# Routed experts of the first layer: two tables of token sums instead of one

## The chip, the core and the metric

The kernel runs on one core of a Trainium2 chip. The metric is device time of one execution in microseconds (us), the median of the runs shown. Engines are named as in the profile: PE is TensorE's matmul and PEld its weight load, DVE is VectorE, ACT is ScalarE, POOL is GpSimd, SP is SyncE, which only issues DMAs and waits here.

## The reference, cut to what matters

The whole program is a two layer model over 1250 tokens (nodes) of 512 float32 values: in each layer a graph network and a linear attention, then a mixture of experts. The change touches the mixture of experts of layer 0:

```python
gate_probs = softmax(x @ gate_w.T)                 # 1250 x 16 experts
top_v, top_i = top_k(gate_probs, 4); top_v = softmax(top_v)
routed = sum over e of combine[:, e] * (gelu(x @ re_w1[e] + re_b1[e]) @ re_w2[e] + re_b2[e])
shared = mean over 2 shared experts of the same form
x = x + routed + shared
```

Each token goes to 4 of 16 experts, so a token's row of the result is a sum of 4 routed terms, the shared term and the residual.

## The kernel before, in words

`build` runs the stages one after the other. Every stage is a block in which each engine has its own instruction stream, and the next stage begins when all engines have left the block. `stage_experts` is called once per layer; it runs `stage_front` (gate, routing tables, shared experts) and then `stage_routed`, which the change edits.

**Tiles.** The front sorts the token and expert pairs by expert and cuts them into tiles of at most 128 pairs of one expert. In layer 0 there are 48 tiles, numbered g = 0 to 47, in layer 1 there are 28. Buffers of a tile exist twice, by its parity b. Tiles 0, 1 and 2 and the last one are written out; the others run in a hardware loop of two tiles per turn on every engine.

**One tile on PE** (in program order of a turn): `raise_up(g)` (L1930, eight matmul records, first product), `turn_hidden(g-1)` (L1939), `turn(g+1)` (L1920, transposes the gathered rows), `bring_down(g-1)` (L1948, second product). On DVE `bias` (L2022) and `place` (L2015, L2016), on ACT `place_hidden` (L1976), `squash` (L1984) and `weigh` (L1990, writes the weighted result `y[b]`).

**One tile on POOL** is the function `tile(i, g, b)`: it reads two numbers of `landed_by` into registers, waits until the gather into `rows[b]` and the add of tile g-2 (same parity) have landed (`landed[b]`), copies the row numbers of tile g (`know_row`, L1854), issues the gather of the token rows of tile g+4 from the DRAM table `token_rows` (`gather`, L1861, which first waits for `place(g+2)`), then waits on both `landed` semaphores for the adds of all tiles of earlier experts, and issues the add of tile g: an indirect DMA that adds the 128 rows of `y[b]` to rows of the DRAM table `token_sums` (`add_rows`, L1869). Within one expert a token occurs once, so adds of one expert touch different rows; adds of different experts can touch the same row, and two such adds in flight together would lose one. `weigh(g)` on ACT waits for `know_row(g)`, which stands behind `landed[b]`, since both overwrite what the add of tile g-2 reads.

**Weights.** SP keeps a ring of 3 experts. `load_expert` (L878, L879, L882; 512 KB, 128 KB and 512 KB) brings expert e when expert e-3 is done.

**Around the loop.** In `stage_adjacency` the DRAM tables are filled with zeros (L594), SP waits for them (L597). At the end of `stage_front` SP writes residual plus shared experts into `token_sums` (L1040). When POOL has seen the last adds land (`all_added`, L1912), SP reads the table back: in layer 0 into `st.res3` (L1845, 125 partitions by 10 rows of 2 KB), in layer 1 into the output (L1847), and waits for it. In layer 0 the next stage is a layer norm (L276 on DVE, L307 on ACT, L300 on PE).

Of the kernel before, what the change touches and what calls it, by code (L numbers as in the profile page):

```python
# [19 lines left out]
F32 = mybir.dt.float32  # L20
# [6 lines left out]
NODES = 1250  # L27
TS = 125
NT = NODES // TS
D = 512  # L30
# [14 lines left out]
ROW = D + NE  # L45
# [35 lines left out]
def stage_semaphores(nc, ctx, cleared=[]):  # L81


    taken = []
    stage = nc.next_id()

    def sem(name):
        taken.append(nc.alloc_semaphore(name=f"{name}_{stage}"))
        return taken[-1]

    def leave():
        while cleared:
            nc.release_semaphore(cleared.pop())
        for s in taken:
            nc.gpsimd.sem_clear(s)
        cleared.extend(taken)

    ctx.callback(leave)
    return sem
# [751 lines left out]
class L0_EXPERTS:  # L851

    top, shared, shared_weight, swiglu = 4, 2, 0.5, False
    slots, early = P, 3
    ff, blocks, w1_cols = 256, 2, 256
    gate_w, gate_b = "L0_ffn_gate_w", None
# [4 lines left out]
class L1_EXPERTS:  # L861

    top, shared, shared_weight, swiglu = 2, 1, 1.0, True
    slots, early = P, 1
    ff, blocks, w1_cols = 384, 3, 768
    gate_w, gate_b = "L1_ffn_gate_w", "L1_ffn_gate_b"
# [917 lines left out]
def stage_routed(nc, st, ar, kind, ins, rt, out):  # L1784
# [5 lines left out]
    TILES = 2 * rt.most_pairs  # L1790
# [7 lines left out]
    hid = [ar.take(F * P) for _ in range(2)]  # L1798
    ht = [ar.take(F * P).rearrange("p (f n) -> p f n", f=F) for _ in range(2)]
    y = [ar.take(D) for _ in range(2)]  # L1800
    weight = ar.take(TILES)
    own_row = [ar.take(2).bitcast(I32) for _ in range(2)]
    if SW:
# [7 lines left out]
    with ExitStack() as ctx:  # L1811
        sem = stage_semaphores(nc, ctx)
        w1_loaded, w2_loaded, sums_read = rt.w1_loaded, rt.w2_loaded, sem("sums_read")
        rows_turned, xt_placed, rows_used = sem("rows_turned"), sem("xt_placed"), sem("rows_used")
        up_ready, up_biased, hid_ready = sem("up_ready"), sem("up_biased"), sem("hid_ready")
        hid_turned, ht_placed, down_ready, y_made = (
# [4 lines left out]
        landed = [nc.alloc_semaphore(name=f"landed{b}_{kind.top}") for b in range(2)]  # L1821
        block = ctx.enter_context(nc.Block())

        def more_pairs(eng):
            return eng.value_load(rt.pairs[0:1, 0:1], min_val=1, max_val=rt.most_pairs - 1)

        def expert_of(eng, g):
            return eng.value_load(rt.expert_of[0:1, bass.ds(g, 1)], min_val=0, max_val=NE - 1)  # L1828
# [1 line left out]
        def ring_of(eng, g):  # L1830
            return eng.value_load(rt.ring_of[0:1, bass.ds(g, 1)], min_val=0, max_val=R - 1)

        sums = rt.sums

        @block.sync
        def _(sp):
            for e in range(kind.early, NE):
                if e >= R:
                    sp.wait_ge(down_ready, sp.value_load(rt.done_by[0:1, e - R:e - R + 1], min_val=1, max_val=TILES + 1))
                load_expert(sp, rt, kind, ins, e)  # L1840
            sp.wait_ge(w1_loaded, 32 * NE)
            sp.wait_ge(w2_loaded, 16 * NE)
            sp.wait_ge(all_added, 1)
            if out is None:
                sp.dma_start(st.res3, sums[1:NODES + 1, :].rearrange("(t p) d -> p t d", p=TS)).then_inc(sums_read, 16)  # L1845
            else:
                sp.dma_start(out, sums[1:NODES + 1, :]).then_inc(sums_read, 16)  # L1847
            sp.wait_ge(sums_read, 16)

        @block.gpsimd  # L1850
        def _(pool):

            def know_row(b, pair):
                pool.tensor_copy(own_row[b], pair).then_inc(row_copied, 1)  # L1854

            def gather(g, b):

                pool.wait_ge(rows_used, g + 3)
                pool.wait_ge(row_copied, g + 2)
                pool.nop().then_inc(gather_begun, 1)  # L1860
                pool.indirect_dma_start(  # L1861
                    out=rows[b], out_offset=None, in_=rt.table,
                    in_offset=bass.IndirectOffsetOnAxis(ap=own_row[b][:, 1:2].bitcast(mybir.dt.uint32), axis=0)
                    ).then_inc(rows_loaded[b], 16)

            def add_rows(g, b):
                pool.wait_ge(y_made, g + 3)
                pool.nop().then_inc(add_begun, 1)  # L1868
                pool.indirect_dma_start(  # L1869
                    out=sums, out_offset=bass.IndirectOffsetOnAxis(ap=own_row[b][:, 0:1].bitcast(mybir.dt.uint32), axis=0),  # L1870
                    in_=y[b], in_offset=None, compute_op=ALU.add).then_inc(landed[b], 16)

            def tile(i, g, b):
                earlier = [pool.value_load(rt.landed_by[odd][0:1, bass.ds(g, 1)], min_val=16, max_val=16 * TILES)  # L1874
                           for odd in range(2)]

                pool.wait_ge(rows_loaded[b], i * 16 + (48 - 16 * b))
                pool.wait_ge(landed[b], i * 16 + (16 - 16 * b))
                know_row(b, rt.row_of[:, bass.ds(g + AHEAD, 1), :].rearrange("p a w -> p (a w)"))
                gather(g, b)  # L1880
                for odd in range(2):
                    pool.wait_ge(landed[odd], earlier[odd])
                add_rows(g, b)

            pool.nop().then_inc(row_copied, 1)
            for b in range(2):

                pool.wait_ge(rows_loaded[b], 16)
                pool.tensor_copy(first_rows[:, b:b + 1], rt.row_of[:, 2 + b, 1:2]).then_inc(first_copied, 1)
                pool.wait_ge(first_copied, b + 1)  # L1890
                pool.wait_ge(rows_used, b + 1)
                pool.indirect_dma_start(
                    out=rows[b], out_offset=None, in_=rt.table,
                    in_offset=bass.IndirectOffsetOnAxis(ap=first_rows[:, b:b + 1].bitcast(mybir.dt.uint32), axis=0)
                    ).then_inc(rows_loaded[b], 16)
            pool.wait_ge(rt.sums_set, 16 * NT)
            for g in range(2):
                know_row(g, rt.row_of[:, g + AHEAD, :])
                gather(g, g)
                if g:  # L1900
                    pool.wait_ge(landed[0], 16)
                add_rows(g, g)
            tile(0, 2, 0)
            more = more_pairs(pool)
            with pool.Fori(1, more) as i:  # L1905
                for b in (1, 0):
                    tile(i, i * 2 + (2 - b), b)
            tile(more, more * 2 + 1, 1)
            for b in range(2):
                pool.wait_ge(landed[b], more * 16 + 16)  # L1910
                pool.wait_ge(rows_loaded[b], more * 16 + 48)
            pool.nop().then_inc(all_added, 1)  # L1912
# [97 lines left out]
        def _(dve):  # L2010
# [16 lines left out]
            def swiglu(g, b):  # L2027
                e = expert_of(dve, g)
                pairs = biased[b].rearrange("p (n m) -> p m n", m=2)
                lo, hi = own_clamp[b][:, 0], own_clamp[b][:, 1]  # L2030
                dve.tensor_copy(own_act[b], rt.act5[:, bass.ds(e * 5, 5)]).then_inc(mixed, 1)
                dve.tensor_copy(own_clamp[b], clamps[:, :, bass.ds(e * 2, 2)]).then_inc(mixed, 1)
                dve.wait_ge(up_biased, g + 3)
                dve.wait_ge(mixed, g * 4 + 2)
                dve.tensor_scalar(gate[b], pairs[:, 0, :], hi[:, 0:1], lo[:, 0:1], ALU.min, ALU.max).then_inc(clipped, 1)
                dve.tensor_scalar(up[b], pairs[:, 1, :], hi[:, 1:2], lo[:, 1:2], ALU.min, ALU.max).then_inc(mixed, 1)
                dve.wait_ge(sig_ready, g + 1)
                dve.scalar_tensor_tensor(out=sig[b], in0=gate[b], scalar=own_act[b][:, 1:2], in1=sig[b],
                                         op0=ALU.mult, op1=ALU.mult).then_inc(mixed, 1)
                dve.wait_ge(mixed, g * 4 + 4)  # L2040
                dve.scalar_tensor_tensor(out=hid[b], in0=up[b], scalar=own_act[b][:, 2:3], in1=sig[b],
                                         op0=ALU.add, op1=ALU.mult).then_inc(hid_ready, 1)
# [9 lines left out]
            with dve.Fori(0, more) as i:  # L2052
                for b in (1, 0):
                    g = i * 2 + (2 - b)
# [6 lines left out]
            g = more * 2 + 1  # L2061
            bias(g, 1)
            if SW:
                swiglu(g, 1)


DYN = 12534
# [2 lines left out]
def build(nc, ins, out):  # L2070
    with ExitStack() as ctx:
        words = 53200
        whole = ctx.enter_context(nc.sbuf_tensor("arena", [P, words], F32))
        st = State()
# [17 lines left out]
        TABLE = P * (-(-(NODES + 1 + P) // P))  # L2092
        st.table = nc.dram_tensor("token_rows", (TABLE, ROW), F32, kind="Internal").ap()
        st.sums = nc.dram_tensor("token_sums", (TABLE, D), F32, kind="Internal").ap()
        st.made_rows = [(st.table, ROW), (st.sums, D)]
        st.routed_zeroed = nc.alloc_semaphore(name="routed_zeroed")


# [1 line left out]
        ar = Arena(whole, st.counts16_at[0], words)  # L2100
# [19 lines left out]
        ar = Arena(whole, DYN, words)  # L2120
# [14 lines left out]
        ar = Arena(whole, DYN, words)  # L2135
# [34 lines left out]
```

## Time and profile before

| | |
|---|---|
| median of 3 runs | 2692.89 us (2692.82 to 2703.66) |
| profiled execution, its own time | 2696.6 us |
| its span, first to last instruction | 2694.8 us |
| mean granted TensorE clock | 0.935 |
| busy: PE, PEld, DVE, ACT, POOL | 84%, 48%, 36%, 19%, 16% |

The profile shows one execution. Its stretches are read by windows in us from the span's start. The routed experts of layer 0 lie at about 990 to 1303, those of layer 1 at about 2400 to 2695. "Issue" as a releaser means that the engine waited for nothing that the profile shows. A releaser is inferred: a wait for several semaphores is put down to the one that came last. Spans on POOL are rough, and some records of matmuls and of DMA landings are missing.

### The profile page before, as it was taken

Reading aid. Unit: us, or ns where it says so; the run is one execution under the profiler, and the core shown is the slowest. Engines: PE = TensorE matmul, PEld = TensorE weight load, DVE = VectorE, ACT = ScalarE, POOL = GpSimd, SP = SyncE. Lnnn points to the kernel's source line nnn. Section 1 sums busy time; section 2 is a strip of 40 time slices with the busy share of each in tenths; the row PEclk is TensorE's granted clock in tenths of the full one; section 3 lists DMA queues with packets and bytes.
Section 4 is the critical chain, followed back from the end, with each engine's and each line's share of the span. In section 5 each row is a group of like instructions: output and inputs, shape, how many; then the busy total and the mean of one; then the engine's idle time right before and its main releaser. Section 6 shows DMA issues by size and latency. Waiting matters only on the chain. (4 is left out here: it accounts for less than half of the span.)

```text
span 2694.8 us, 27626 instructions
## 1 busy us (share of the span) xinstructions
PE 2270.1 (84%) x7356; PEld 1284.5 (48%) x7357; DVE 971.8 (36%) x2322; ACT 501.8 (19%) x885; POOL 442.6 (16%) x599
## 2 busy tenths in 40 slices
PE   4976775989897898877498698998989988889996
PEld 2532332444444445444244246883458854435553
DVE  4162665420203632211105435531245402624443
ACT  1110122101010302222200014421134302201111
POOL 3995000000000014444100000000000010002332
PEclk9987998999999999999698898998999999989998
DMA  3000200000000326666300000002000010237774
GB/s 109 0 0 0 87 0 16 16 1 16 0 0 0 125 64 161 149 154 134 105 0 0 30 25 1 1 1 85 1 0 1 0 35 22 96 129 207 233 233 126
DMA packets 77350, 159.33 MB, mean 59 GB/s; under 512 B 9219, under 2 KB 20526, under 8 KB 77202
## 3 DMA queue, kind: packets, MB, share of 16 engines
q1 hardware_dynamic: 59602, 115.62, 12.8%
q0 software_dynamic: 17664, 42.64, 7.9%
q8 instruction: 47, 0.77, 0.1%
q14 instruction: 37, 0.30, 0.0%
HBM read 122.06 MB, written 38.74 MB: 60 GB/s over the span
## 5 line engine op out<-in xcount | busy, mean ns | idle before, releaser
L1692 PE MATMUL bank<-arena 125*125 125x257 f32 x1600 | 355.8, 383 | 4.8 <-DVE arena L1611 4.8
L1692 PEld LDWEIGHTS bank<-arena 125*125 125x125 f32 x1600 | 302.2, 189 | 60.5 <-DVE arena L1611 6.3
L1930 PE MATMUL bank<-arena 128*128 x832 | 250.9, 452 | 25.4 <-issue 12.6
L795 PE MATMUL bank<-arena 125*128 125x500 f32 (+1 forms) x720 | 252.6, 512 | 2.3 <-ACT arena L825 2.3
L1930 PEld LDWEIGHTS bank<-arena 128*128 128x128 f32 x832 | 157.0, 194 | 141.3 <-issue 81.8
L1507 PE MATMUL bank<-arena 128*125 128x512 f32 x480 | 211.3, 600 | 9.1 <-DMA arena<-in_L_gnn_W 9.1
L1948 PE MATMUL bank<-arena 128*128 x360 | 177.3, 622 | 36.3 <-ACT arena L1976 27.9
L795 PEld LDWEIGHTS bank<-arena 125*128 125x128 f32 x720 | 135.8, 189 | 120.5 <-issue 110.6
L382 POOL TENSOR_SCALAR arena<-arena 125x125 bf16<-125x125 f16 x320 | 184.4, 760 | 40.7 <-POOLq L266 40.7
L2022 DVE TENSOR_TENSOR arena<-bank,arena 128x384 f32<-128x384 f32 (+1 forms) x104 | 51.5, 496 | 307.8 <-PE bank L1930 296.2
L637 PE MATMUL bank<-arena 125*125 125x500 bf16 x416 | 122.8, 418 | 45.7 <-DVE arena L613 45.7
L1670 ACT ACTIVATE arena<-arena 125x625 f32<-125x625 f32 x160 | 134.5, 900 | 102.5 <-DVE arena L1611 102.3
L429 PE MATMUL bank<-arena 128*125 128x512 f32 x320 | 143.6, 603 | 10.0 <-DMA arena<-in_L_mix_Wqkv 9.3
L1507 PEld LDWEIGHTS bank<-arena 128*125 128x125 f32 x480 | 90.7, 191 | 123.3 <-issue 113.3
L1869 POOL DMA_INDIRECT token_sums<-arena x76 | 121.2, 1595 | 156.8 <-DMA token_sums<-arena 111.9
L613 DVE TENSOR_SCALAR arena<-arena 125x500 bf16<-125x500 f16 x416 | 119.0, 346 | 59.9 <-PE bank L637 53.7
L1611 DVE SCALAR_TENSOR_TENSOR arena<-arena 125x625 f32<-125x625 f32 x160 | 132.4, 864 | 15.8 <-ACT arena L1670 15.8
L777 PE MATMUL bank<-arena 128*125 128x512 f32 x240 | 111.6, 627 | 21.6 <-DVE arena L733 21.6
L752 DVE TENSOR_TENSOR arena<-bank,arena 128x500 f32<-128x500 f32 (+1 forms) x36 | 21.3, 592 | 291.7 <-PE bank L795 291.7
L1543 DVE CUSTOM_DVE_ANT_0 arena<-arena 125x256 f32<-125x256 f32 x160 | 58.6, 421 | 185.7 <-ACT arena L1530 169.3
L1044 POOL MEMSET arena<- 125x20 f32 (+1 forms) x2 | 0.2, 117 | 740.0 <-POOLq L266 740.0
L1739 POOL TENSOR_TENSOR arena<-arena 125x5120 f32<-125x5120 f32 x1 | 11.0, 10999 | 636.5 <-DMA arena<-in_L_gnn_bfc 636.5
(313 smaller groups left out, 2462.8 us busy)
## 6 DMA issues: line engine op xcount, KB each, us to landing
arena<-in_L_ffn_expert_w SPq DMA_DIRECT2D x16, 1536.0 KB
arena<-in_L_ffn_re_w SPq DMA_DIRECT2D x32, 512.0 KB
arena<-in_L_ffn_expert_w SPq DMA_DIRECT2D x16, 768.0 KB
arena<-in_L_ffn_expert_b SPq DMA_DIRECT2D x16, 384.0 KB
token_rows<-arena SPq DMA_DIRECT2D x2, 2500.0 KB
token_sums<-arena SPq DMA_DIRECT2D x20, 250.0 KB
arena<-in_L_gnn_W SPq DMA_DIRECT2D x1, 4096.0 KB, 13.1
arena<-in_L_mix_Wqkv SPq DMA_DIRECT2D x3, 1024.0 KB, 5.3
```

What stands on the lines that cost most here:

```text
L382: pool.tensor_scalar(st.low_marks[:, c, :], st.iota16[:, 0:TS], st.low[:, c:c + 1], None, ALU.is_equal)
L429: last = pe.matmul(out[0:TS, :], st.turned[:, k, i * TS:(i + 1) * TS], w3[:, k, j * D:(j + 1) * D], start=(k == 0), stop=(k == KT - 1))
L613: dve.tensor_scalar(marks[:, u, :], st.iota16[:, 0:WIN * NT], float(w * WIN * NT), st.key[:, bass.ds(col, 1)], ALU.add, ALU.is_equal).then ...
L637: pe.matmul(bank, stays, marks[:, u, :], start=False, stop=False, skip_group_check=True).then_inc(marks_free, 1)
L795: last = pe.matmul(st.bank[4 + n % 4][:, 0:cn], h[:, s, f * P:(f + 1) * P], st.counts[:, s, c0:c0 + cn], start=(s == 0), stop=(s == NT - 1))
L1507: last = pe.matmul(st.bank[n % 4][0:TS, :], x, w[:, k, half * 512:(half + 1) * 512], start=(k == 0), stop=(k == K - 1))
L1611: dve.scalar_tensor_tensor(out=prob[:, u % 2, s, :], in0=excess[:, n % EXCESS, :], scalar=by_one[:, s, head:head + 1], in1=st.counts16[:, ...
L1670: act.activation(excess[:, n % EXCESS, :], row[:, head, d0:d0 + HALF], ACT.Relu, scale=by_fifth[:, s, head:head + 1], bias=minus_one[:, s, ...
L1692: return pe.matmul(st.bank[n % OUTS][0:TS, 0:ONCOL], prob[:, u % 2, s, j * TS:(j + 1) * TS], st.slots[:, head + 1, s, :], start=(s == 0), ...
L1869: pool.indirect_dma_start(out=sums, out_offset=bass.IndirectOffsetOnAxis(ap=own_row[b][:, 0:1].bitcast(mybir.dt.uint32), axis=0), in_=y[b] ...
L1930: last = pe.matmul(st.bank[UP[b][h]][:, 0:WP], xt[b][:, k, :], rt.ring[:, bass.ds(r, 1), k * W + h * WP:k * W + (h + 1) * WP].rearrange("p ...
L1948: last = pe.matmul(st.bank[DOWN[b]], ht[b][:, f, :], rt.ring[:, bass.ds(r, 1), W2_AT + f * D:W2_AT + (f + 1) * D].rearrange("p a n -> p (a ...
```

## The change

`stage_routed` of layer 0 adds tiles of even parity to `token_sums` and tiles of odd parity to a second DRAM table, `more_sums`. Tiles no longer wait for the adds of earlier experts; the wait on `landed[b]` for tile g-2, of the same parity and so of the same table, stays. At the end SP reads both tables in two halves each, and at the end of DVE's stream ten additions put the second table's rows to those of the first. `more_sums` is made and zeroed with the other tables. Layer 1 keeps one table, its waits and its read.

```diff
 class L0_EXPERTS:
...
+    sum_tables = 2
...
 class L1_EXPERTS:
...
+    sum_tables = 1
...
+    more_sums = ar.take(NT * D, TS).rearrange("p (t d) -> p t d", t=NT) if kind.sum_tables == 2 else None
+        half_read = [sem(f"half_read{h}") for h in range(2)]
-        sums = rt.sums
+        TWO = kind.sum_tables == 2
+        sums = [rt.sums, st.more_sums if TWO else rt.sums]
+        HALF = NT // 2
             if out is None:
-                sp.dma_start(st.res3, sums[1:NODES + 1, :].rearrange("(t p) d -> p t d", p=TS)).then_inc(sums_read, 16)
+                for h in range(2):
+                    for b, to in enumerate((st.res3, more_sums)):
+                        sp.dma_start(to[:, h * HALF:(h + 1) * HALF, :],
+                                     sums[b][1 + h * HALF * TS:1 + (h + 1) * HALF * TS, :].rearrange(
+                                         "(t p) d -> p t d", p=TS)).then_inc(half_read[h], 16)
             else:
-                sp.dma_start(out, sums[1:NODES + 1, :]).then_inc(sums_read, 16)
-            sp.wait_ge(sums_read, 16)
+                sp.dma_start(out, sums[0][1:NODES + 1, :]).then_inc(sums_read, 16)
+                sp.wait_ge(sums_read, 16)
...
-                    out=sums, out_offset=bass.IndirectOffsetOnAxis(ap=own_row[b][:, 0:1].bitcast(mybir.dt.uint32), axis=0),
+                    out=sums[b], out_offset=bass.IndirectOffsetOnAxis(ap=own_row[b][:, 0:1].bitcast(mybir.dt.uint32), axis=0),
...
-                earlier = [pool.value_load(rt.landed_by[odd][0:1, bass.ds(g, 1)], min_val=16, max_val=16 * TILES)
+                earlier = [] if TWO else [pool.value_load(rt.landed_by[odd][0:1, bass.ds(g, 1)], min_val=16, max_val=16 * TILES)
                            for odd in range(2)]
...
-                for odd in range(2):
-                    pool.wait_ge(landed[odd], earlier[odd])
+                for odd, tiles in enumerate(earlier):
+                    pool.wait_ge(landed[odd], tiles)
                 add_rows(g, b)
...
-                if g:
+                if g and not TWO:
                     pool.wait_ge(landed[0], 16)
...
+            if out is None:
+                for t in range(NT):
+                    dve.wait_ge(half_read[t // HALF], 32)
+                    dve.tensor_tensor(st.res3[:, t, :], st.res3[:, t, :], more_sums[:, t, :], ALU.add)
...
+        st.more_sums = nc.dram_tensor("more_sums", (TABLE, D), F32, kind="Internal").ap()
-        st.made_rows = [(st.table, ROW), (st.sums, D)]
+        st.made_rows = [(st.table, ROW), (st.sums, D), (st.more_sums, D)]
```

## Rows read from the trace of the kernel before

**Rows 1.** Busy by stretch of the loop: engines, granted clock, DMA share, GB/s.

```profile
core 0: us, PE busy (x) PEld busy (x) DVE busy (x) ACT busy (x) POOL busy (x), PEclk, DMA share, GB/s
1003.80:1264.50 260.70, 212.23 (x810) 128.89 (x810) 52.93 (x135) 65.38 (x136) 126.26 (x136) 0.99 0.67 151
```

**Rows 2.** Waits in 1000:1290: who waited for whom, total us, times, longest.

```profile
POOL token_sums L1869 <- DMA token_sums<-arena: 81.4, 31, 6.7
ACT arena L1990 <- POOL arena L1854: 58.2, 16, 5.3
POOL arena L1861 <- DVE arena L2016: 27.3, 17, 7.2
POOL arena L1854 <- DMA token_sums<-arena: 3.5, 5, 1.6
```

**Rows 3.** Timeline of PE, first product of tiles: start, us, idle before.

```profile
1003.77 1.99 PE L1930 MATMUL bank<-arena 128*128 x8
...
1009.49 1.99 PE L1930 MATMUL bank<-arena 128*128 x8 [0.87 <-issue]
...
1031.12 1.99 PE L1930 MATMUL bank<-arena 128*128 x8 [0.50 <-issue]
...
1036.11 1.99 PE L1930 MATMUL bank<-arena 128*128 x8
...
1199.85 1.99 PE L1930 MATMUL bank<-arena 128*128 x8 [0.21 <-DMA arena<-in_L_ffn_re_b]
...
1208.63 1.89 PE L1930 MATMUL bank<-arena 128*128 x8
...
1237.13 1.99 PE L1930 MATMUL bank<-arena 128*128 x8
...
1264.52 1.99 PE L1930 MATMUL bank<-arena 128*128 x8 [0.74 <-issue]
```

**Rows 4.** Timeline of POOL around one load of weights, with SP's issue of it.

```profile
1041.80 1.59 POOL L1869 DMA_INDIRECT token_sums<-arena  x1 [5.11 <-DMA token_sums<-arena]
...
1045.80 1.60 POOL L1869 DMA_INDIRECT token_sums<-arena  x1 [0.30 <-DMA token_sums<-arena]
1046.83 0.76 POOL L1854 COPY arena<-arena 128x2 int32 x1
...
1052.80 0.37 SPq L878 DMA_DIRECT2D arena<-in_L_ffn_re_w  x1
...
1054.56 1.59 POOL L1869 DMA_INDIRECT token_sums<-arena  x1 [1.03 <-DMA token_sums<-arena]
1055.92 0.43 POOL L1854 COPY arena<-arena 128x2 int32 x1
1058.28 1.01 POOL L1861 DMA_INDIRECT arena<-token_rows,arena  x1 [1.93 <-DVE arena L2016]
1064.54 1.59 POOL L1869 DMA_INDIRECT token_sums<-arena  x1 [5.25 <-DMA token_sums<-arena]
1066.25 0.18 POOL L1854 COPY arena<-arena 128x2 int32 x1
1067.24 1.01 POOL L1861 DMA_INDIRECT arena<-token_rows,arena  x1 [0.80 <-POOL arena L1854]
1068.55 1.60 POOL L1869 DMA_INDIRECT token_sums<-arena  x1 [0.30 <-issue]
```

**Rows 5.** Line L1869, the adds: time from issue to landing where recorded.

```profile
DMA to landing us min/median/max: 4.5/8.5/9.3
```

**Rows 6.** Timeline of the end of the stage, all engines.

```profile
1275.15 1.60 POOL L1869 DMA_INDIRECT token_sums<-arena  x1 [0.30 <-issue]
1280.52 0.33 SPq L1845 DMA_DIRECT2D arena<-token_sums  x1
1303.15 1.28 ACT L307 ACT_TABLE_LOAD   x1 [29.27 <-PEq L1811]
1303.19 1.28 DVE L276 BATCH_NORM_STATS2 arena<-arena 125x6 f32<-125x512 f32 x2 [36.10 <-PEq L1811]
```

**Rows 7.** Transfers in 1281:1304: DMA share in tenths and GB/s, 40 slices.

```profile
DMA  0123333333333333333333333333333333333000
GB/s 21 28 71 114 118 125 132 132 128 125 125 128 135 128 125 125 125 132 132 128 125 125 132 132 128 125 125 128 135 128 125 125 125 132 132 128 118 11 0 0
DMA packets 1255, 2.56 MB, mean 111 GB/s; under 512 B 5, under 2 KB 5, under 8 KB 1255
```

**Rows 8.** Three loads of 500 KB to 125 partitions, issued together; transfers in 1545:1565.

```profile
1543.05 0.41 SPq L1473 DMA_DIRECT2D arena<-in_L_gnn_a_src  x1
1543.51 0.34 SPq L1473 DMA_DIRECT2D arena<-in_L_gnn_a_dst  x1
1543.89 1.54 SPq L1475 DMA_DIRECT2D arena<-in_L_gnn_b  x1
...
DMA  8999999996333333333333333333333320000000
GB/s 328 410 410 410 426 434 418 410 401 279 131 131 131 123 131 131 123 131 131 131 123 131 131 131 123 131 131 123 139 131 131 131 107 25 0 0 0 0 0 0
```

**Rows 9.** Groups of DVE by shape: additions in SBUF, busy us, mean ns.

```profile
L1601 DVE TENSOR_TENSOR arena<-arena 125x500 f32<-125x500 f32 x16 | 10.6, 670 | 0.0
L1249 DVE TENSOR_TENSOR arena<-arena 125x576 f32<-125x576 f32 x1 | 0.8, 759 | 0.1
```

**Rows 10.** Zeroing of the tables: issues with KB and us to landing; SP's waits.

```profile
token_rows<-arena SPq DMA_DIRECT2D x1, 2904.0 KB, 9.5
token_sums<-arena SPq DMA_DIRECT2D x1, 2816.0 KB, 16.3
...
SPq L583 <- PEq L583: 168.3, 1, 168.3
SPq L583 <- DMA token_sums<-arena: 15.0, 1, 15.0
```

**Rows 11.** Gap and restart of PE behind the stage: the same columns as rows 1.

```profile
1281.00:1303.00 22.00, 0.00 (x0) 0.00 (x0) 0.00 (x0) 0.00 (x0) 0.00 (x0) 0.50 0.30 116
1311.00:1330.00 19.00, 13.59 (x76) 11.57 (x76) 4.80 (x11) 9.86 (x18) 0.00 (x0) 0.74 0.47 140
```

## Prediction

> **What bounds the kernel now.** The stage is found first by the lines it uses, then read by windows. Over the loop of layer 0 PE is busy 212 of 261 us, with a few records missing, at a granted clock of 0.99, while POOL is busy 126 and the DMA engines 0.67 [rows 1]. So PE is the engine with the most work, but it isn't full. The table of waits says why not: POOL sat 81.4 us in 31 waits before its adds until earlier adds had landed, and behind it ACT's `weigh` waited 58.2 us in 16 cases for POOL's copy of row numbers [rows 2]. That total is tempting, and it is not the gain. The 81.4 us lie on POOL, which has slack; what counts is how much later PE starts its tiles.
>
> The timeline of PE gives that. The first product of tile 2 starts at 1003.77 and that of tile 47 at 1264.52 [rows 3], 45 intervals in 260.75 us, 5.79 us each. I listed all of them. Thirty-three are 4.87 to 5.85 us long, mean 5.39; the other twelve are 6.16 to 8.78 us and sum to 82.8 us. The longest is 1199.85 to 1208.63, and the last stretch, 1237.13 to 1264.52, has five intervals of 5.48 us on average [rows 3]. The twelve long ones come about once per expert, each behind a stall of POOL of 4 to 6.7 us such as the 5.25 us before the add at 1064.54 [rows 4]. The pattern: SP issues the next expert's weights at 1052.80, the add of the last tile of the expert follows at 1054.56, shares the DMA engines with them, and lands just before 1064.54. The longest recorded landing is 9.3 us [rows 5]. An add without a load beside it is quicker: that of 1041.80 had landed when the copy started at 1046.83, within 5.0 us [rows 4].
>
> **The change part by part.**
>
> *Removed: the wait for earlier experts.* If the long intervals become like the others, the loop takes 45 x 5.39 = 242.6 us, 18.1 less. Taking the last stretch, where no weights come in, 45 x 5.48 = 246.6, 14.1 less. I take 16. The ends: the shortest common interval is 1031.12 to 1036.11, 4.99 us [rows 3]; if every tile ran so, the loop would take 224.6 and the gain would be 36. In most intervals, though, PE idles 0.5 to 0.9 us before L1930 for "issue" [rows 3], which names no wait on POOL. At the other end the gain is nothing. What is late next is PE itself, at about 5.4 us a tile. The two register loads per tile of POOL that go are hidden: POOL needs about 4 us per tile, 1041.80 to 1045.80 [rows 4].
>
> *Kept: the wait for tile g-2.* It stands before the copy of tile g, and the gather of tile g+4, the add of tile g and ACT's `weigh(g)` are queued behind it. With an interval of 5.4 us, the add of g-2 is 10.8 us before the add of g. Behind the copy POOL needs 0.2 us, a pause of 0.8, the gather of 1.0 and a pause of 0.3 before it can add (1066.25 to 1068.55, [rows 4]), 2.3 us. So a landing within 8.5 us costs nothing, and one at 9.3 to 10 us makes the add 0.8 to 1.5 us late once per expert. `weigh` would then be about half a us late, and PE asks for that result one tile later, so most of it is covered. For 13 loads I take 1 us in all, between 0 and 13 x 0.8 = 10 us. Gain: 16 - 1 = 15 us.
>
> *Added: the second table to read, on the path.* Nothing else runs between the last add and the next layer norm. The add at 1275.15 is followed by the read at 1280.52, and DVE starts the layer norm at 1303.19 [rows 6]. In between 2.56 MB move at 125 to 132 GB/s with a DMA share of 0.3 [rows 7]: five of sixteen engines' worth, not all. At 128 GB/s a table takes 20.0 us. The question is whether reads of the second table use the same five. Three loads with the same 125 partitions, issued within a us, show it: once the 16 engine transfer ahead of them is through, they go on at 131 GB/s and a share of 0.3 [rows 8]. They share. So two tables take 40.0 us, 20.0 more. Ends: 0 (if the second ran on other engines) and 20.5 (the rate of the slower slices).
>
> The Trainium skill, page "DMA: Bandwidth & Descriptors", section "Why a DMA increments its semaphore by 16 and not by 1", gives the reason: a DMA issued from SP runs on the largest number up to 16 that divides its slowest dimension, 5 for 125 partitions, and always on the lowest-numbered engines. By that rule, too, all four reads go through the same five, and splitting them in halves wins no rate. The trace agrees with its 0.3 of rows 7 and 8; had the engines been free to choose, this term would be near 0 and the sum negative.
>
> *Added: ten additions on DVE.* Shapes of 125x500 take 670 ns and 125x576 take 759 ns in SBUF [rows 9], so 125x512 takes about 0.69 us. The first five run while the second half of the tables is read, 20 us long; if that cover were gone they would cost 3.5. The last five wait for the last byte: 5 x 0.69 = 3.5 us, plus 0.2 to start. Ends by the two shapes 3.4 and 3.8, with the start 3.4 to 4.2. The SP issues of three more DMAs, 0.33 us each [rows 6], lie under the transfer of the first.
>
> *Added: zeroing.* The second zeroed table landed 6.8 us after the first [rows 10], so a third costs SP some 7 us, at a place where SP afterwards waits 168.3 us for PE. Nobody else waits for it. Cost 0, with 168 us of cover.
>
> *The rest.* Two semaphores more to clear per stage, also in layer 1, whose loop is otherwise the same: 0 to 0.3 us. PE's pause grows from 38 to some 60 us. The clock was already at its lower level of 1.2 GHz (0.50) in this pause, and the restart shows 0.74 on average [rows 11]; a longer pause at the same level should restart alike, 0, at most 1.
>
> **Sum.** Read +20.0, DVE +3.7, loop -15, together +8.7 us. On the profiled execution: span 2694.8 to 2703.5, own time 2696.6 to 2705.3. That execution is 3.7 us above the median of the three runs, so the predicted median is 2692.9 + 8.7, about 2701.5.
>
> **The rivals.**
>
> *The wait for tile g-2 takes the place of the removed one* (slower). Price: up to the whole 16 us; the time would be 2692.9 + 23.7 - (0 to 10), 2707 to 2717. It decides once a landing beside a weight load passes about 10.5 us, or gathers, issued behind the same wait, come too late for PE's transposes. For it: landings of 9.3 and almost 10 us [rows 5, 4], with the 8.5 us of slack already used up, and adds that now follow each other closer. Against it: the DMA engines have a third of their time free [rows 1], and `weigh` has one tile of slack. Chance 0.23.
>
> *PE reaches its own floor.* If the 0.5 to 0.9 us of "issue" before L1930 come from POOL's lateness after all, the gain is between 21 and 36 us: 2680 to 2695. For it: the intervals of 4.9 to 5.0 exist. Against it: the last stretch, without weights in flight, has none. Chance 0.17.
>
> *The second read runs on other engines.* The cost shrinks to 3.7: 2692.9 + 3.7 - 15, some 2682. Against it stand the three loads of rows 8; for it, that reads from DRAM rows aren't broadcasts like those. Chance 0.05.
>
> **How the numbers follow.** The forecast, a gain of 10 to 21 and a cost of 23.7, gives 2695.6 to 2706.6 with chance 0.55. 0.5% of the time, about what a measurement of this kernel can tell from no change, is 13.5 us: bounds 2679.4 and 2706.4. Slower is the first rival, 0.23. Faster needs the far end of PE's floor, or the second read elsewhere with a good loop: 0.04. The rest, 0.73, is within. The range of 2688 to 2714 leaves out the top of the first rival (0.05), the lower half of the second (0.08) and the third (0.05).
>
> **What would show it.** In the changed trace: POOL's wait before L1869 for landed adds gone from 81.4 to some 15 us or less; POOL's copy L1854 waiting for landed adds more than the 3.5 us of rows 2; intervals of L1930 at 5.3 to 5.5 us without the twelve long ones, and the first product of tile 47 about 15 us earlier; from the first read's issue to the layer norm 46 us instead of 22.7, at a DMA share of 0.3 all through; five additions of 0.69 us at its end. It is wrong if the share during the reads is 0.6, if long intervals stay with `weigh` waiting for L1854, or if the loop runs at 5.0 us a tile.

## The result, and the profile after

The changed kernel takes 2716.88 us (median of 7 runs, 2713.06 to 2722.63), the kernel before 2693.59 in its 7 runs. The ratio is 1.0078 with an interval of 1.006 to 1.0095: 16 to 26 us slower, outside the range of 2688 to 2714, where the forecast was 8.7 us slower. The profiled execution of after took 2715.25 us, 18.7 more than that of before; the sum below is made between these two.

The end of the stage took as long as was worked out. Timeline of the kernel after, the last stretch, all engines, to set beside [rows 6]:

```profile
1273.88 0.34 SPq L1855 DMA_DIRECT2D arena<-token_sums  x1
...
1287.69 10.31 SPq L1855 DMA_DIRECT2D arena<-more_sums  x1
1296.57 3.10 DVE L2080 TENSOR_TENSOR arena<-arena 125x512 f32<-125x512 f32 x5 [35.50 <-DMA arena<-more_sums]
1316.80 3.10 DVE L2080 TENSOR_TENSOR arena<-arena 125x512 f32<-125x512 f32 x5 [17.14 <-DMA arena<-more_sums]
1320.17 1.28 ACT L307 ACT_TABLE_LOAD   x1 [52.51 <-PEq L1814]
```

Transfers of after in 1274:1320, share in tenths and GB/s, as in [rows 7]:

```profile
DMA  1233333333333333333333333333333333331000
GB/s 14 77 128 128 128 128 128 126 130 126 128 128 126 126 126 123 125 125 125 126 125 126 130 126 125 128 128 126 123 125 123 125 125 125 125 125 69 0 0 0
DMA packets 2520, 5.12 MB, mean 111 GB/s; under 512 B 20, under 2 KB 20, under 8 KB 2520
```

From the first read's issue to ACT's first instruction of the layer norm it is 1273.88 to 1320.17, 46.3 us, against 22.6 in [rows 6]: 23.7 more, at a share of 0.3 all through. The additions take 0.62 us each, five of them hidden. Up to the second five additions it is 42.9 us (1273.88 to 1316.80), 20.3 more than the whole of before; these additions and the step to ACT add 3.4.

The loop didn't come out as forecast. Timeline of PE, kernel after, the first products (L1942 now), with three neighbours in the middle:

```profile
1002.39 1.99 PE L1942 MATMUL bank<-arena 128*128 x8
...
1019.58 1.99 PE L1942 MATMUL bank<-arena 128*128 x8 [0.94 <-DMA arena<-in_L_ffn_re_b]
1025.19 1.99 PE L1942 MATMUL bank<-arena 128*128 x8 [0.76 <-issue]
1030.94 1.99 PE L1942 MATMUL bank<-arena 128*128 x8 [0.89 <-issue]
...
1258.49 1.99 PE L1942 MATMUL bank<-arena 128*128 x8 [0.98 <-issue]
```

Tile 2 to tile 47 take 256.1 us instead of 260.75 [rows 3]: 4.65 us less, where 15 were forecast. The twelve long intervals are gone, the longest is now 6.0 us. But the short ones are gone too: all 45 lie between 5.27 and 5.99, 5.69 on average. Waits of after in 1000:1285 (engine, tile and line, who ended the wait: us in total, times, longest):

```profile
POOL arena L1873 <- DVE arena L2028: 88.5, 44, 7.0
...
PE bank L1942 <- issue: 26.9, 33, 1.1
...
PE bank L1942 <- DMA arena<-in_L_ffn_re_b: 10.4, 12, 1.1
POOL more_sums L1881 <- DMA token_sums<-arena: 2.9, 3, 1.0
```

POOL's 81.4 us of waiting for landed adds [rows 2] are gone. The 2.9 us listed are three pauses of up to 1.0 us before adds of odd tiles, a place where the changed program has no wait for adds, so that releaser is a wrong guess of the profile; the copy of row numbers, which does stand behind the wait for tile g-2 (L1866 now), isn't listed with any wait for an add. POOL now waits for DVE, which waits for PE. And PE pauses before 45 first products, 37 us in all. Sum of the two profiled executions: before tile 2 -1.4 us, loop -4.65, from the last first product to the read -0.6, read and additions +23.7, behind it +1.6: together +18.65. Outside the stage the code is the same but for the second table's zeroing.

**What PE does in the pause.** Its sequencer reads the next tile's expert and ring place from memory into registers before the first product (`expert_of` L1832, `ring_of` L1835 of after). For one tile, first the add issued ahead of them, from POOL's timeline of after:

```profile
1020.34 1.59 POOL L1881 DMA_INDIRECT more_sums<-arena  x1 [0.98 <-issue]
```

Instructions of L1832 of after in 1022:1024.5 (count: ns min/median/max, first and last start):

```profile
L1832 PEldq TENSOR_LOAD <-arena x1: 935/935/935, 1022.7 to 1022.7; - x1
```

Instructions of L1835 of after in the same stretch:

```profile
L1835 DVEq TENSOR_LOAD <-arena x1: 808/808/808, 1022.8 to 1022.8; - x1
```

A register load mostly takes 0.3 us here. The two that were under way at 1023 took 0.94 on PE and 0.81 on DVE and ended together, at 1023.65, 3.3 us after the start of the add's issue at 1020.34. The next took 0.31. Below are all register loads of PE and DVE in 1000:1285 of each trace, sorted by the time since the start of the last add's issue (long means over 450 ns):

| kernel | begun 2.05 to 2.9 us after an add: long of all | median end of the long ones, us after the add | begun outside 2.0 to 3.3 us: long of all |
|---|---|---|---|
| before | 34 of 38 | 3.31 | 2 of 229 |
| after | 88 of 89 | 3.31 | 0 of 188 |

So a register load of another engine that is under way while an add is some 2.3 to 3.3 us old is mostly held until the add is 3.3 us old. Before, GpSimd's add was delayed by waits of changing length, so the loads met the held stretch sometimes: of the loads ahead of first products of tiles 3 to 47, 18 were long. After, nothing but `weigh` sets the add, and `weigh` follows the second product: the add is issued about 2.5 us before PE's next register load in nearly every tile, and 44 are long. The waits' removal locked the two into the worst phase.

**What a tile of PE is made of.** The intervals alternate, 5.61 and 5.75 above, for a second reason. The loop has two tiles per turn, and ahead of the first of them PE's sequencer goes back to the loop's start. Instructions of L1970 of after in 1024.5:1031, the loop's end between two tiles:

```profile
L1970 PEldq COMPARE_BRANCH  x1: 208/208/208, 1028.3 to 1028.3; - x1
```

If from every interval the time is taken off by which its four PE register loads exceed 0.305 us each, the 22 intervals of after without the loop's end come to 4.98 us (spread 0.01) and the 23 with it to 5.37 (spread 0.03). So PE's pace with these loads in place, and none held, is 5.17 us on average or 233 us for the loop, and the held loads make up the other 23 us of the 256.1. Of the 37 us of pause 23 are the hold, some 9 the loop's end.

**The theories for the runs.** A: this hold sets the pace of 5.7 us. B (rival, that of the prediction): the wait for tile g-2 and the landings set it, and long loads are a sign only. C: PE's sequencer has a fixed overhead, whatever POOL does.

### The profile page after: what moved, and what is told of

Same layout as the page of the kernel before. It is cut to its first block and busy times, and to the rows that moved or that the text cites. A ratio compares the mean times of both kernels' runs of the same rounds, so it can differ in the third digit from the quotient of the medians.

```text
span 2713.4 us, 27231 instructions
## 1 busy us (share of the span) xinstructions
PE 2264.7 (83%) x7356; PEld 1282.4 (47%) x7357; DVE 978.6 (36%) x2332; ACT 502.6 (19%) x885; POOL 444.7 (16%) x599
## 5 line engine op out<-in xcount | busy, mean ns | idle before, releaser
L1942 PE MATMUL bank<-arena 128*128 x832 | 250.6, 451 | 42.5 <-issue 26.9
L1942 PEld LDWEIGHTS bank<-arena 128*128 128x128 f32 x832 | 156.1, 194 | 158.1 <-issue 98.6
L300 PE MATMUL bank<-arena 125*128 125x125 f32 x160 | 26.9, 350 | 111.0 <-DVE arena L290 111.0
```

The source lines that it names most:

```text
L1942: last = pe.matmul(st.bank[UP[b][h]][:, 0:WP], xt[b][:, k, :], rt.ring[:, bass.ds(r, 1), k * W + h * WP:k * W + (h + 1) * WP].rearrange("p ...
```

## The experiments

Times are medians; ratios are to the kernel before on the same chip, whose median was 2693.6 to 2697.8 us. "Loop" is from the first product of tile 2 to that of tile 47 in the profiled execution.

| run | what | ratio (interval) | median us | loop us |
|---|---|---|---|---|
| before | | 1 | 2693.59 | 260.8 |
| after | | 1.0078 (1.006 to 1.0095) | 2716.88 | 256.1 |
| e1_tail_alone | only the second table's read | 1.0103 (1.0081 to 1.0125) | 2723.16 | 262.7 |
| e2_loop_alone | only the loop | 0.999 (0.998 to 0.9999) | 2692.89 | 257.3 |
| e3_numbers_early | after, register loads early | 1.0017 (1.0002 to 1.0032) | 2700.43 | 240.1 |
| e4_before_numbers_early | before, register loads early | 0.9963 (0.9947 to 0.998) | 2685.58 | 255.1 |
| e5_add_later | after, adds delayed | one run | 2737.30 | 269.4 |
| e6_split_reads | after, reads split | 1.0011 (1.0 to 1.0022) | 2699.59 | 257.0 |
| e8_both | after, early and split | 0.9945 (0.9926 to 0.9965) | 2680.88 | 236.4 |
| e9_before_both | before, early and split | 0.9925 (0.9901 to 0.995) | 2677.65 | 253.2 |
| e10_gather_first | e8 with gathers ahead of the wait | 0.9972 (0.996 to 0.9984) | 2689.47 | 248.3 |
| e11_plain_odd | after, odd tiles write plainly | one run | 2699.18 | 243.1 |
| e13_before_gather_first | e9 with gathers ahead of the wait | 1.0011 (0.9991 to 1.0031) | 2701.59 | 276.6 |

### The two halves of the change

e1: waits and the single target of before, with the second table's zeroing, read and additions.

```diff
-                earlier = [] if TWO else [pool.value_load(
+                earlier = [pool.value_load(
-                if g and not TWO:
+                if g:
-                    out=sums[b], out_offset=
+                    out=sums[0], out_offset=
```

> The changed kernel with the waits of before put back and every tile added to the first table; the second table is zeroed, read and added as in the change. The tail theory (four reads of 125 partitions share five engines): from the first read's issue to the layer norm about 46 us instead of 22.7, time 23 to 24 us above before, and the loop as before, tile 2 to tile 47 in 261 us. If the loop's change had cost time of its own, or the larger zeroing did, this would be well under 20 us above before or well over 26.

e2: the loop of the change, the old read.

```diff
-                for h in range(2):
-                    for b, to in enumerate((st.res3, more_sums)):
...
+                sp.dma_start(st.res3, sums[0][1:NODES + 1, :].rearrange("(t p) d -> p t d", p=TS)).then_inc(sums_read, 16)
+                sp.wait_ge(sums_read, 16)
...
-                    dve.wait_ge(half_read[t // HALF], 32)
-                    dve.tensor_tensor(st.res3[:, t, :], st.res3[:, t, :], more_sums[:, t, :], ALU.add)
```

> The changed kernel's loop with two tables, but only the first is read back, in one transfer, and nothing is added on VectorE: the terms of the odd tiles are left out of the result. If the loop gained 4.7 us, as the trace of after has it, the time is 3 to 7 us under before; if the loop had gained the 15 us forecast and something else took it, 15 us under.

e1's profile has 46.3 us from read to layer norm once more (1281.19 to 1327.49) and a loop like before's, 2 us longer. Timed, it is 28 us slower, with an interval of 22 to 34 that takes in the 24 expected. e2 is 0.3 to 5.4 us faster: the loop alone is worth 3 us or so, not 15. Its loop of 257.3 us is after's in the trace, too. The costs are where they were thought to be; the gain is missing.

### Register loads moved

e3: two loads per tile instead of four, into registers kept per parity, ahead of the second product, none ahead of the first.

```diff
+            def fetch(g, to):
+                pe.reg_load(to[0], rt.expert_of[0:1, bass.ds(g, 1)])
+                pe.reg_load(to[1], rt.ring_of[0:1, bass.ds(g, 1)])
...
             def raise_up(g, b):
-                e, r = expert_of(pe, g), ring_of(pe, g)
+                e, r = numbers(b)
...
             def bring_down(g, b):
-                e, r = expert_of(pe, g), ring_of(pe, g)
+                e, r = numbers(b)
...
                     turn(g + 1, 1 - b, i * 16 + 32)
+                    fetch(g + 1, spare)
                     bring_down(g - 1, 1 - b)
+                    for to, new in zip(ahead[1 - b], spare):
+                        pe.reg_mov(to, new)
```

> The changed kernel, with TensorE's two register loads for the next tile moved ahead of the second product and kept in registers, so two loads per tile instead of four, none between the products. Theory A (a register load that is under way 2.3 to 3.3 us after the issue of an add is held until 3.3 us, and with the waits gone this falls on the loads ahead of every first product): the pause of 0.85 us before the first product goes, a tile takes 5.0 to 5.1 us, the loop 225 to 232 us instead of 256, time 24 to 31 us under after. Theory B (the wait for tile g-2 and the landing of adds set the pace, and long register loads are a sign of it only): a tile stays at 5.7 us and the time at after's. The same in layer 1 for both, where up to 10 us more can go.

Timeline of PE, e3 (L1951 is the first product, L1932 the transposes):

```profile
1017.95 1.89 PE L1951 MATMUL bank<-arena 128*128 x8
...
1022.54 1.89 PE L1951 MATMUL bank<-arena 128*128 x8
...
1032.33 1.89 PE L1951 MATMUL bank<-arena 128*128 x8
...
1036.65 0.66 PE L1932 MATMUL bank<-arena 128*128 128x128 f32 x4 [2.21 <-DMA arena<-token_rows,arena]
...
1041.88 1.89 PE L1951 MATMUL bank<-arena 128*128 x8
```

The pause is gone: an undisturbed tile takes 4.59 us, less than the 5.0 that theory A gave, since not only the hold but the loads and the loop's end, too, now lie under the second product. The time falls by 0.6%, some 16 us, less than the 24 to 31 expected. Theory B is out as the pace of after. A next limit shows: six intervals are 7.8 to 9.6 us long, such as 1032.33 to 1041.88. That is why the loop is 240 and not the 225 to 232 expected. Timeline of POOL and SP, e3, at that place:

```profile
1027.93 0.38 SPq L880 DMA_DIRECT2D arena<-in_L_ffn_re_w  x1
1028.89 1.01 POOL L1873 DMA_INDIRECT arena<-token_rows,arena  x1 [0.80 <-POOL arena L1866]
...
1038.80 0.18 POOL L1866 COPY arena<-arena 128x2 int32 x1 [3.01 <-DMA more_sums<-arena]
```

Landing of the gather of 1028.89 (L1873 in 1028.5:1029.5), and all engines in 1038.3:1041.7 (columns as in [rows 1]):

```profile
DMA to landing us min/median/max: 7.7/7.7/7.7
1038.30:1041.70 3.40, 3.23 (x4) 1.51 (x5) 0.00 (x0) 0.00 (x0) 1.19 (x2) 0.50 0.31 51
```

In all six PE waits 1.7 to 2.2 us for gathered rows, as at 1036.65. The gather in question was issued 1.0 to 1.1 us after the next expert's weights and took 7.4 to 7.7 us to land, where the shortest take 3.3. PE then waits 1.1 to 1.4 us more before its second product, and in five of the six the granted clock falls behind this idle time to its lower level, 0.50 or 1.2 GHz, for 3.4 us. The wait of POOL's copy for the add of tile g-2, at 1038.80, ended after PE had gone on at 1036.65, so it isn't what PE waited for; whether such waits earlier on, such as the 2.6 us before the copy at 1024.01, put the gathers beside the weights is not shown. Layer 1's loop didn't gain.

e4 is the same edit on before.

> The kernel before (one table, all waits), with the same move of TensorE's register loads as in the last experiment. There the change's loop took 235.5 us with six stalls of some 4.5 us. Theory A: before also gains, since 27 of its loads were long, but less than after did, because the waits for earlier experts now bind: loop 245 to 258 us instead of 261, time 3 to 16 us under before. If the waits were the only limit of before: no gain, 261.

Loop 255.1, time 5 to 14 us under before. (The 235.5 us that the expectation gives for e3's loop leave out its first interval.) Before, too, paid for the loads, but its waits bind: twelve intervals stay long. With the loads out of the way the change's loop is 15 us shorter than before's, 240.1 against 255.1. The size is that of the prediction, but not its tiles: six long intervals instead of none, and short ones of 4.8 us instead of 5.4.

### The add moved

e5: 1.5 us of idle work on GpSimd ahead of each add.

```diff
                 pool.wait_ge(y_made, g + 3)
+                if TWO:
+                    pool.nop().then_inc(idle_begun, 1)
+                    pool.iota(idle_row, pattern=[[1, 1600]], base=0, channel_multiplier=0,
+                              allow_small_or_imprecise_dtypes=True).then_inc(idled, 1)
+                    pool.wait_ge(idled, g + 1)
                 pool.nop().then_inc(add_begun, 1)
```

> The changed kernel with an idle instruction of some 1.5 us on GpSimd ahead of every add of layer 0, which moves the add against TensorE's register loads and changes nothing on TensorE. Theory A: the loads ahead of the first product are over before the add's 2.3 us are, long loads (over 450 ns) there fall from 43 to under 10, a tile takes 5.1 to 5.5 us though GpSimd has more to do. Theory B: adds land 1.5 us later, so a tile takes as long or longer, 5.7 to 6.5 us. Theory C (TensorE's sequencer has a fixed overhead per tile and the add's time doesn't matter): 5.7 us.

Timeline of PE, e5, first products (L1949):

```profile
1030.73 1.99 PE L1949 MATMUL bank<-arena 128*128 x8 [0.50 <-issue]
...
1036.02 1.99 PE L1949 MATMUL bank<-arena 128*128 x8
...
1043.56 1.99 PE L1949 MATMUL bank<-arena 128*128 x8 [0.48 <-issue]
```

Ahead of first products 1 load is long instead of 44, where A gave under 10; another 25 are long ahead of second products. The idle time before first products falls from 37 to 12 us, no more than the 14 that are left of after's 37 without the hold, and common intervals are 5.3 to 5.4 us, within A's 5.1 to 5.5. That is against C as to the hold; the other 14 us are a fixed overhead of PE's sequencer, as C has it. But thirteen intervals are 6.4 to 8.8 us long: POOL's stream is now full and its copies, on which `weigh` waits, come late (184 us of waits for L1868 against 2.5 after). The loop as a whole is slower, 269 us, as B has it. So the pause follows the add, but what the hold is worth in time can't be read from this run; the next run tells.

e11: odd tiles write instead of add, so that even and odd tiles differ within one run.

```diff
-                    in_=y[b], in_offset=None, compute_op=ALU.add).then_inc(landed[b], 16)
+                    in_=y[b], in_offset=None, **({} if TWO and b else dict(compute_op=ALU.add))).then_inc(landed[b], 16)
```

> The changed kernel where the adds of odd tiles write their rows to the second table instead of adding them (the same indirect DMA without its addition), so sums of odd tiles are left out. Which part of the add holds register loads? If it is the addition: after writes of odd tiles the loads take 0.3 us, long loads on TensorE fall from 43 to about 22 and tiles alternate between 5.0 and 5.7 us, loop some 240 us. If it is any indirect DMA out of the on-chip memory: 43 long loads, 256 us. Even tiles are the control in the same run.

Timeline of POOL, e11, the add of an even tile and the plain write of an odd one:

```profile
1016.82 1.62 POOL L1881 DMA_INDIRECT token_sums<-arena  x1 [0.74 <-issue]
...
1021.81 1.00 POOL L1881 DMA_INDIRECT more_sums<-arena  x1 [0.95 <-DMA arena<-token_rows,arena]
```

Timeline of PE, e11, first products of three tiles:

```profile
1015.25 1.99 PE L1942 MATMUL bank<-arena 128*128 x8
...
1020.99 1.99 PE L1942 MATMUL bank<-arena 128*128 x8 [0.88 <-DMA arena<-in_L_ffn_re_b]
...
1025.96 1.99 PE L1942 MATMUL bank<-arena 128*128 x8
```

The intervals alternate, 5.7 with an add and 5.0 with a plain write, through the whole loop. Not all of that is the write: the tiles with an add are also those with the loop's end, 0.39 us. The fair comparison is with the same tiles of after. The 22 intervals with a plain write fall from 5.55 to 5.04 us on average, the 23 with an add stay (5.82 and 5.75). The loop is 243.1 us, 13 less than after's, and the one run is 18 us under after's median. Of loads begun 2.05 to 2.9 us after an add 27 of 28 are long, after a plain write 7 of 43. The plain write isn't free of it: nineteen loads of DVE begun 1.4 to 1.7 us after one took 0.5 to 0.8 us and ended 1.9 to 2.3 us after it, and the seven ended at 2.7 to 3.1. Its issue takes 1.0 us instead of 1.6. So it isn't the addition alone that holds, as one branch of the expectation had it: both do, at different times after the issue, and mostly only the add's falls on PE's loads. Theory A stands by this: nothing but the DMA of every other tile was changed, and most of the held time went in just those.

### The reads

e6: each read in one of 112 and one of 13 partitions.

```diff
-                        sp.dma_start(to[:, h * HALF:(h + 1) * HALF, :],
...
+                        for p0, p1 in ((0, 112), (112, TS)):
+                            sp.dma_start(to[p0:p1, h * HALF:(h + 1) * HALF, :], rows_of[p0:p1]).then_inc(half_read[h], 16)
```

> The changed kernel, each of its four reads cut into one of 112 partitions and one of 13, so that a transfer can be spread over 16 and 13 engines. If the number of partitions confines a read to five engines, the reads run at 300 to 400 GB/s, take 13 to 18 us instead of 40, and the time is 22 to 27 us under after, at or a little under before. If the rate of 128 GB/s comes from the table's rows in DRAM, nothing changes.

Busy time of e6 by stretch (columns as in [rows 1]) while it reads:

```profile
1276.50:1299.50 23.00, 0.00 (x0) 0.00 (x0) 3.10 (x5) 0.00 (x0) 0.00 (x0) 0.50 0.97 223
```

All engines are busy now, 0.97 instead of 0.3, so the number of partitions was what confined the read to a few engines. But 5.12 MB move at 223 GB/s, not at 300 to 400: five engines made 128, sixteen don't make three times that; what limits the rate then stays open. From read to layer norm 27.7 us instead of 46.3, time 18 us under after where 22 to 27 were expected. The share follows the rule of the Trainium skill, "DMA: Bandwidth & Descriptors", "Why a DMA increments its semaphore by 16 and not by 1", by which 112 partitions go to 16 engines; the rate is what this run shows.

### Both, and one edit too many

> The changed kernel with TensorE's numbers read early and the split reads. The two terms lie one behind the other, so they should add: 16 us and 22 to 27 us under after, which is 13 to 20 us under before, faster by 0.5 to 0.75%.

> The kernel before with both edits, numbers early and its one read split in the same way. The read falls from 20 to 7 us, so 13 us under the kernel before with early numbers alone. If the change to two tables is worth something once its costs are cut, the changed kernel with both edits is faster than this one by the loops' difference (10 to 22 us) less 10 us for the second read and its additions.

Both beat before, by 0.55% and 0.75%; their intervals overlap, so two tables and one can't be told apart here. e8 is 15 us under before, within the 13 to 20 expected; e9 is 8 us under e4, not 13, since its read is 7.5 us shorter and not 13. e8's loop is 17 us shorter than e9's, and its end 12.8 us longer (28.0 against 15.2). That favours e8 by 4 us, and the profiled executions take the same time all the same, because outside the stage e8's lost as much: from the layer norm to layer 1's loop it took 4.2 us more. That stretch runs the same code in all thirteen profiles and took 1122 to 1132 us, so differences of a few us between two profiled executions say nothing about the stage.

e10 and e13 put POOL's gather ahead of the wait for tile g-2, with a copy of its own:

```diff
                 pool.wait_ge(rows_loaded[b], i * 16 + (48 - 16 * b))
-                pool.wait_ge(landed[b], i * 16 + (16 - 16 * b))
-                know_row(b, rt.row_of[:, bass.ds(g + AHEAD, 1), :].rearrange("p a w -> p (a w)"))
+                know_from(b, rt.row_of[:, bass.ds(g + AHEAD, 1), :].rearrange("p a w -> p (a w)"))
                 gather(g, b)
+                pool.wait_ge(landed[b], i * 16 + (16 - 16 * b))
+                know_row(b, rt.row_of[:, bass.ds(g + AHEAD, 1), :].rearrange("p a w -> p (a w)"))
```

> The changed kernel with numbers early and split reads, and in GpSimd's stream the gather of tile g+4 now comes ahead of the wait for the add of tile g-2, with a copy of row numbers of its own. Theory: what is left once the register loads are out of the way is that wait, six stalls of 4 to 5 us with late gathers behind it. Then the gathers come in time, the stalls shrink to under 2 us, loop from 236 to 215 to 225 us and 10 to 20 us under the same kernel without this. If the stalls come from the DMA engines being full, it stays within 3 us.

> The same edit on the kernel before with numbers early and its read split: its waits for earlier experts still stand between a gather and the add, and hold the next gather. So less is won than in the changed kernel, 0 to 8 us; the loop stays at 245 to 253 us. If the changed kernel wins 10 to 20 us and this one less than 8, two tables are worth their second read in this setting: the changed one is then faster by 5 us or more.

Both expectations missed: loops 12 and 23 us longer than without the edit. Waits of e10 in 1000:1270, columns as above:

```profile
ACT arena L2030 <- POOL arena L1868: 172.8, 43, 5.1
...
POOL token_sums L1886 <- ACT arena L2030: 39.6, 23, 2.9
POOL more_sums L1886 <- ACT arena L2030: 38.4, 23, 3.2
```

`weigh` needs the copy of row numbers, and that copy now stands behind a gather that itself waits for DVE. The edit took one wait from the gather and laid a longer one on `weigh`, in 43 tiles (13 in e8, 40 us), and the add then waits for `weigh`. Eight intervals over 6 us remain in e10, seven of them with PE waiting for gathered rows, and near none of them did POOL's copy wait over 1 us for an add. So the wait for tile g-2 wasn't what made the gathers late there. The idea behind the edit was wrong.

## Why the prediction was wrong, point by point

- *Read of the second table, +20.0, same five engines; additions, +3.7:* right. It is 20.3 and 3.4 us, at 123 to 130 GB/s; the two small misses cancel in the 23.7 us. e1 has the same. The rival of a read on other engines is out.
- *Zeroing hidden, layer 1 unchanged:* no run contradicts it. Layer 1's intervals are those of before.
- *Loop, -15:* the step that failed; it measured -4.65. The prediction took the mean of the 33 ordinary intervals, 5.39 us, for PE's own pace ("What is late next is PE itself, at about 5.4 us a tile"), and put the pause before the first product down to nothing that could change, since it "names no wait on POOL". No wait it is, but it is POOL's doing. The long intervals did become like the others, but the others became longer: 5.39 was a mixture, eleven tiles without a held load at 5.09 us on average and twenty-two with one or two at 5.54, and removing the waits put nearly all tiles under the hold, at 5.69. That is 13.5 us over the loop, against the 18.1 that the twelve long intervals cost. The stretch at the end of before's loop, taken for the lower estimate because no weights came in, averaged 5.48 with a held load in each of its five tiles. e5 and e11 show what switches between the values.
- *The wait for tile g-2 as the slower rival:* the side was right, the mechanism wrong, and that the time of 2716.9 lies in its band of 2707 to 2717 is luck. POOL's copy waited for no landed add after. Once the loads were early some adds did land late, up to 9.2 us after their issue in e3, but in the six long intervals PE waited for gathered rows that landed late.
- *PE's own floor of 5.0, if POOL's lateness caused the pause:* the question was put the wrong way round. POOL's being on time causes most of it. Nor is 5.0 a floor for every tile: with the loop's end it is 5.37, so the loop couldn't have come to 224.6 us but to 233. With the loads early the floor is 4.59 us (e3).
- *Range:* the forecast case had a gain of 10 to 21 us. A gain near zero was allowed for only through the g-2 wait, up to 2717, and the range of 2714 cut it.

What stays open is how the issue of such a DMA holds register loads. The runs show when, not what is shared. And of the 23 us between the medians the profiled pair shows 18.7, the rest being the spread of the executions.

## What to carry to other kernels

A pause marked "issue" on the busiest engine is not a constant: look at what its sequencer does there, above all at register loads and the loop's end, and at what other engines do at that moment. When two kinds of tile are compared within one run, check that they don't differ in something else, such as their place in the loop. Removing a wait also fixes a phase, and the new phase has to be worked out and not averaged from the old one. Before a second transfer is put on the path, check on how many DMA engines the first one runs; here the partition count of 125 cost the two tables 18.6 us (46.3 against 27.7), and the loop won 15 to 17 at best (e3 against e4, e8 against e9).

## What the runs showed of the hardware

- A register load from on-chip memory takes 0.30 us, and up to 1.1 us if under way between about 2.3 and 3.3 us after GpSimd starts to issue an indirect add of 128 rows of 2 KB; in before and after most held loads of PE and DVE end 3.3 us after that start. Behind a plain indirect write the holds end at 1.9 to 2.3 or 2.7 to 3.1 us (e11).
- The end of a hardware loop's turn costs PE 0.39 us where it isn't hidden behind a product (5.37 against 4.98 us a tile in after), its branch alone 0.21.
- A read of 125 partitions runs at a share of 0.3 of the DMA engines and 128 GB/s, four such reads queued together as well; 112 and 13 partitions fill the engines to 0.97 and reach 223 GB/s (e6).
- A gather issued 1 us after a load of weights took 7.4 to 7.7 us to land, the quickest of the loop 3.3 (e3).
- Five DVE additions of 125x512 in float32 take 3.10 us, 0.62 each, where the 670 ns of 125x500 [rows 9] would make 3.4 of them.
